# A four-layer network on one core: who makes the inputs of the 64-state scan, and where both scans put their results

## The reference

```python
deltaA = jnp.exp(delta[..., None] * A[None, None])
dBu = delta[..., None] * B_ssm[:, :, None, :] * u[..., None]
_, h = jax.lax.associative_scan(_scan_comb, (deltaA, dBu), axis=1)     # h = deltaA * h_before + dBu
y = jnp.einsum('bldn,bln->bld', h, C_ssm) + u * D_param
```

## Time and profile before

| | us |
|---|---|
| median of the runs | 10314.9 |
| profiled execution | 10319.8 |
| its span | 10318.0 |
| stage two (64-state scan), 2838 to 5845 | 3007 |
| stage four, forward half, 6913 to 8561 | 1648 |
| stage four, backward half, 8561 to 10228 | 1667 |
| VectorE, ScalarE, GpSimd, TensorE busy of the span | 8275.2, 8166.8, 5747.3, 9215.3 |

### The profile page before, as it was taken

One profiled execution on the slowest core, in us unless ns is written; L12 is line 12 of the kernel. 1 busy time (PEld: TensorE's weight loads), 2 busy tenths in 40 slices (PEclk: granted clock), 3 DMA queues, 4 the chain that ended last, 5 costly groups with the idle time before them and its releaser, 6 DMA issues. The chain is left out here.

```text
span 10318.0 us, 146585 instructions
## 1 busy us (share of the span) xinstructions
PE 9215.3 (89%) x50532; PEld 4668.1 (45%) x50532; DVE 8275.2 (80%) x7254; ACT 8166.8 (79%) x15277; POOL 5747.3 (56%) x2628
## 2 busy tenths in 40 slices
PE   9999999999888888888888899988899998888885
PEld 6767767767533333333333344433333333333332
DVE  7858858668499999999999711129999999999997
ACT  5646646556499999999999655569999999999995
POOL 0000000000088888888888500029999999999996
PEclk9999999999899999999999999999999999999997
DMA  0000000000055555555555300015556566656666
GB/s 39 0 1 0 0 1 0 0 0 0 9 182 180 189 183 180 186 182 181 182 184 185 121 8 8 8 63 188 197 193 198 193 199 195 199 193 200 196 196 224
DMA packets 338551, 1249.79 MB, mean 121 GB/s; under 512 B 39280, under 2 KB 39408, under 8 KB 334448
## 3 DMA queue, kind: packets, MB, share of 16 engines
q1 hardware_dynamic: 338032, 1243.13, 37.0%
HBM read 1144.40 MB, written 56.62 MB: 116 GB/s over the span
## 5 line engine op out<-in xcount | busy, mean ns | idle before, releaser
L1905 POOL TENSOR_TENSOR l_ring<-l_ring 128x1024 f32<-128x1024 f32 x1024 | 2450.2, 2422 | 159.0 <-DVE l_ring L1983 158.0
L1001 POOL TENSOR_TENSOR l_hc<-l_h,l_hc 128x1024 f32<-128x1024 f32 x1024 | 2218.1, 2182 | 535.5 <-DVE l_h L1099 517.8
L1983 DVE TENSOR_TENSOR_SCAN l_ring<-l_ring,l_carry,l_ps 128x1024 f32<-128x1024 f32 x960 | 2199.6, 2333 | 0.9
L1099 DVE TENSOR_TENSOR_SCAN l_h<-l_decay,l_h,l_ps 128x1024 f32<-128x1024 f32 x768 | 1755.1, 2333 | 17.0 <-ACT l_decay L873 4.9
L116 POOL COPY l_qm<-l_q 128x128 f32 x128 | 82.4, 646 | 2576.4 <-PE l_ps L188 2179.9
L889 ACT ACTIVATE l_xt<-l_duT,l_BT 128x128 f32<-128x128 f32 x4736 | 1441.2, 388 | 11.1 <-PE l_ps L705 10.9
L1795 ACT ACTIVATE l_xt<-l_duT,l_BT 128x128 f32<-128x128 f32 x4096 | 1247.1, 390 | 0.0
L1587 PE MATMUL l_ps<-l_ring,w_sb 64*64 64x512 f32 x8192 | 1179.1, 648 | 0.8 <-PE l_ps L1587 0.4
L722 PE MATMUL l_ps<-l_hc,w_sb 64*64 64x512 f32 x8192 | 1148.4, 632 | 2.3 <-POOL l_hc L1001 1.8
L212 PE MATMUL l_ps<-l_attnT,l_vT 128*128 128x128 f32 x8192 | 1095.7, 277 | 1.3 <-ACT l_attnT L283 1.3
L212 PEld LDWEIGHTS l_ps<-l_attnT,l_vT 128*128 128x128 f32 x8192 | 1013.9, 192 | 137.8 <-issue 114.7
(11 more groups left out here) (238 smaller groups left out, 14865.6 us busy)
## 6 DMA issues: line engine op xcount, KB each, us to landing
l_hc<-l_rows_dram SPq DMA_DIRECT2D x1024, 512.0 KB, 4.7
l_ring<-l_rows_dram SPq DMA_DIRECT2D x1024, 512.0 KB, 5.1
l_crossed<-l_delta SPq DMA_DIRECT2D x160, 256.0 KB, 3.8
l_gate_dram<-l_gate SPq DMA_DIRECT2D x32, 512.0 KB, 6.6
l_recon_dram<-l_recon SPq DMA_DIRECT2D x32, 512.0 KB, 6.5
l_gate<-l_gate_dram SPq DMA_DIRECT2D x32, 512.0 KB, 5.6
l_xw<-x_dram SPq DMA_DIRECT2D x30, 513.5 KB, 6.8
x_dram<-x SPq DMA_DIRECT2D x16, 512.0 KB, 2.6
```

The lines of the kernel that those rows point to most:

```text
L1001: nc.gpsimd.tensor_tensor(hc[:, unit % CS, :], h[:, unit % HS, window(unit)][:, along(K)], hc[:, unit % CS, :], ALU.mult).then_inc(hc_done, 1)
L1099: nc.vector.tensor_tensor_scan(h[:, unit % HS, window(unit)][:, along(K)], decay[:, unit % DS, :], odd_in if odd else even_in, before, ALU ...
L1905: nc.gpsimd.tensor_tensor(hc[:, unit % CS, :], h[:, unit % HS, :], hc[:, unit % CS, :], ALU.mult).then_inc(hc_done, 1)
L1983: nc.vector.tensor_tensor_scan(h[:, unit % HS, order], decay[:, unit % DS, order], x_now[:, order], before, ALU.mult, ALU.add).then_inc(sc ...
```

## The change

It has these parts.

1. `TURNED` grows from 5 to 14 even units of stage two, whose input ScalarE and TensorE now make instead of TensorE's broadcast and VectorE's multiplication. `BT` grows from 37 to 46 columns.
2. A new list `MADE` names 14 odd units of stage two whose transposed input GpSimd makes, in one operation of 128x1024 (`odd_input`), instead of eight activations on ScalarE. It stands ahead of the two products of the pair before. A semaphore `xt_made` counts them; `xt_ready` counts only ScalarE's.
3. Where a unit's result goes in its slot: in both stages the first column is now 4 (n // 2) + n % 2 plus 1 or 2, so that it is 2 or 3 modulo 4 where the product reads along the positions, and 1 or 2 modulo 4 where it reads in reverse. A slot of `h` has 64 columns more than 1024 in stage two and 32 in stage four.
4. Stage four takes over stage two's way of the carry: `h` is a tensor of its own, results are written forward and in reverse by turns, the next chunk's scan starts from the column that is still there, and `carry`, `keep` and its semaphore go.
5. The scratch space of the software DMA queue is halved, and GpSimd waits once for `taps_ready` (the convolution's taps lie in `xt` until then).

```diff
 DT_AT = PARTS * SEL
-TURNED = (6, 13, 20, 24, 29)
+TURNED = (1, 2, 3, 5, 7, 8, 9, 11, 15, 18, 25, 26, 29, 31)
+MADE = (0, 1, 3, 5, 8, 9, 13, 14, 15, 18, 19, 21, 29, 31)
+FIRST_TURNED = min([(k, 0) for k in TURNED] + [(k, 1) for k in range(S1 // 2) if k not in MADE])
 BTW = SEL + len(TURNED)
...
         rows_dram = nc.dram_tensor("l1_rows_dram", [NCH * S1, CH], F32, kind="Internal").ap()
-        h = sb("h", [128, HS, CH + 2 * USES])
+        h = sb("h", [128, HS, CH + 4 * USES])
         hc = sb("hc", [128, CS, CH])
...
         b_mm = sem("b_mm"); inp_done = sem("inp_done"); xt_ready = sem("xt_ready"); xt_mm = sem("xt_mm")
+        xt_made = sem("xt_made")
         decay_ready = sem("decay_ready"); scan_done = sem("scan_done")
...
             K, q = divmod(unit, S1)
-            first = q // HS if K % 2 else 2 * USES - 1 - q // HS
+            n = q // HS if K % 2 else 2 * USES - 1 - q // HS
+            first = 4 * (n // 2) + n % 2 + (1 if K % 2 else 2)
             return slice(first, first + CH)
...
             return 2 * (P + turned_before(P)) + (2 if odd and P % PAIRS in TURNED else 0)
+
+        def made_before(P):
+            return P // PAIRS * len(MADE) + sum(k < P % PAIRS for k in MADE)
...
                 at_least(pe, scan_done, 2 * P + odd - 1)
+                by_pool = odd and P % PAIRS in MADE
+                if by_pool:
+                    pe.wait_ge(xt_made, made_before(P) + 1)
                 for hf in range(2):
-                    pe.wait_ge(xt_ready, n + hf + 1)
+                    if not by_pool:
+                        pe.wait_ge(xt_ready, n + hf + 1 - 2 * made_before(P))
                     for t in range(4):
...
                 K, k = divmod(P, PAIRS)
-                if k == 0:
+                if (k, odd) == FIRST_TURNED:
                     act.wait_ge(duT_out, 2 * K + 2)
...
             decays(0, 0)
-            turned_input(0, 1, 0)
+            if 0 not in MADE:
+                turned_input(0, 1, 0)
             decays(1, 0)
...
                         decays(2 * P + 2, own)
-                        turned_input(P + 1, 1, own)
+                        if (k + 1) % PAIRS not in MADE:
+                            turned_input(P + 1, 1, own)
                         decays(2 * P + 3, own)
...
+            def odd_input(P, p):
+                K, k = divmod(P, PAIRS)
+                if k == MADE[0]:
+                    pool.wait_ge(duT_out, 2 * K + 2)
+                    pool.wait_ge(bt_ready, K + 1)
+                n = halves_before(P, 1)
+                at_least(pool, xt_mm, n + 2 - XS)
+                into = xt[:, n % XS:n % XS + 2, :].rearrange("p s (t d) -> p (s t) d", d=128)
+                nc.gpsimd.tensor_tensor(into, duT[:, p, :, :], BT[:, p, :, k:k + 1].broadcast_to([128, BLK, 128]),
+                                        ALU.mult).then_inc(xt_made, 1)
+
             squares(0, 0)
...
             input_rate(0, 0)
+            pool.wait_ge(taps_ready, 1)
+            if 0 in MADE:
+                odd_input(0, 0)
             for K in range(NCH):
                     P = K * PAIRS + k
+                    if P + 1 < NCH * PAIRS and (k + 1) % PAIRS in MADE:
+                        odd_input(P + 1, p if k + 1 < PAIRS else 1 - p)
                     product(2 * P)
...
     HS, DS, CS, XS = 4, 4, 8, 4
+    USES = TI * S3 // HS
     ctx = ExitStack()
...
         taps = sb("taps", [128, K3, DI])
-        ring = sb("ring", [128, (HS + DS + CS) * CH])
+        h = sb("h", [128, HS, CH + 4 * USES])
+        ring = sb("ring", [128, (DS + CS) * CH])
         slots = lambda at, n: ring[:, at * CH:(at + n) * CH].rearrange("p (s n) -> p s n", s=n)
-        h, decay, hc = slots(0, HS), slots(HS, DS), slots(HS + DS, CS)
+        decay, hc = slots(0, DS), slots(DS, CS)
         xw = sb("xw", [128, 3, CH + PAD])
...
         loaded = sb("loaded", [128, CH])
-        carry = sb("carry", [128, TI * S3])
         zero = sb("zero", [128, 1])
...
         b_mm = sem("b_mm"); inp_done = sem("inp_done"); xt_ready = sem("xt_ready"); xt_mm = sem("xt_mm")
-        decay_ready = sem("decay_ready"); scan_done = sem("scan_done"); kept = sem("kept")
+        decay_ready = sem("decay_ready"); scan_done = sem("scan_done")
         c_in = [sem(f"c_in_{i}") for i in range(CS)]
...
         forward = lambda K: K < NCH
-
-        def keeps_before(P):
-
-            d, i = divmod(P, NCH * TI * PAIRS)
-            kept_pairs = (NCH - 1) * TI * PAIRS
-            return 2 * (d * kept_pairs + min(i, kept_pairs))
+        in_time = lambda K: forward(K) == (K % 2 == 0)
+
+        def window(unit):
+
+            K, i = divmod(unit, TI * S3)
+            n = i // HS if K % 2 else 2 * USES - 1 - i // HS
+            first = 4 * (n // 2) + n % 2 + (2 if in_time(K) else 1)
+            return slice(first, first + CH)
+
+        def last_column(unit):
+            own = window(unit)
+            return own.start if unit // (TI * S3) % 2 else own.stop - 1
...
                     pool.wait_ge(scan_done, unit + 1)
-                    nc.gpsimd.tensor_tensor(hc[:, unit % CS, :], h[:, unit % HS, :], hc[:, unit % CS, :],
-                                            ALU.mult).then_inc(hc_done, 1)
+                    K = unit // (TI * S3)
+                    along = slice(None) if in_time(K) else slice(None, None, -1)
+                    nc.gpsimd.tensor_tensor(hc[:, unit % CS, :], h[:, unit % HS, window(unit)][:, along],
+                                            hc[:, unit % CS, :], ALU.mult).then_inc(hc_done, 1)
...
                         dve.wait_ge(inp_done, P + 1)
-                        at_least(dve, kept, keeps_before(P - 1) if P else 0)
                     dve.wait_ge(decay_ready, unit + 1)
                     at_least(dve, hc_done, unit - HS + 1)
-                    before = carry[:, e * S3 + q:e * S3 + q + 1] if K % NCH else zero[:]
+                    into = slice(None, None, -1) if K % 2 else slice(None)
+                    at = last_column(unit - TI * S3) if K % NCH else 0
+                    before = h[:, unit % HS, at:at + 1] if K % NCH else zero[:]
                     x_now = odd_in if odd else even_in
-                    nc.vector.tensor_tensor_scan(h[:, unit % HS, order], decay[:, unit % DS, order], x_now[:, order],
-                                                 before, ALU.mult, ALU.add).then_inc(scan_done, 1)
-
-                def keep(unit):
-                    S, q = divmod(unit, S3)
-                    K, e = divmod(S, TI)
-                    at = CH - 1 if forward(K) else 0
-                    dve.wait_ge(scan_done, unit + 1)
-                    nc.vector.tensor_copy(carry[:, e * S3 + q:e * S3 + q + 1], h[:, unit % HS, at:at + 1]).then_inc(kept, 1)
+                    nc.vector.tensor_tensor_scan(h[:, unit % HS, window(unit)][:, into], decay[:, unit % DS, order],
+                                                 x_now[:, order], before, ALU.mult, ALU.add).then_inc(scan_done, 1)
...
                         even_input(P + 1)
-                    if S // TI % NCH < NCH - 1:
-                        keep(2 * P)
-                        keep(2 * P + 1)
                     pieces(S, r)
...
     arrays = {name: _np.ascontiguousarray(a) for name, a in arrays.items()}
-    nc = _bacc.Bacc("TRN2", target_bir_lowering=False, num_devices=1)
+    nc = _bacc.Bacc("TRN2", target_bir_lowering=False, num_devices=1, dynamic_dma_scratch_size=8192)
     args = [nc.dram_tensor(name, a.shape, mybir.dt.from_np(a.dtype), kind="ExternalInput").ap()
```

## The result

The changed kernel takes 10187.5 us (median of 4 runs, 10180.4 to 10189.7) against 10312.0 for the kernel before: 0.9875 of its time, 95% interval 0.9863 to 0.9886. That is 127 us under the 10314.9 that the forecast started from; forecast was 222 us less, and the time lies 2.5 us inside the upper end of the range of 10040 to 10190.

| | before | after | forecast change |
|---|---|---|---|
| stage two | 3006.0 | 2874.8 | -150 |
| stage four, forward half | 1648.1 | 1642.1 | -19 |
| stage four, backward half | 1666.2 | 1672.5 | -53 |

A forecast was written before the change was run, and what follows sets the result against it. VectorE's chain bounds stage two; in stage four ScalarE bounds the forward half and VectorE, with stalls, the backward. 10319.8 - 150 (stage two) - 72 (stage four) = 10097.8, profiled 4.9 above the runs' median, so 10093; range 10040 to 10190.

The forecast's parts named there:

- The products, 1.96 to 2.00 us at the new places: GpSimd, both stages: every product takes the cheap form; stage two's come to 125.4 us a chunk instead of 137.
- The new operation at 1.96 us: GpSimd, stage two: each of 14 odd inputs a chunk costs as much as a cheap product.
- Stage two, 9.4 us a chunk: 64-state scan: 187.9 us a chunk falls to 178.5, saving 150 us over 16 chunks.
- The ideal saving of 11.2: VectorE, stage two: 9 even inputs of 1.25 us leave each chunk, 187.9 to 176.7 us.
- The 1.8 us booked for waits: Stage two, per chunk: 0.3 for TensorE's transposes, 0.5 for late odd inputs, 1.0 for rows of C.
- The wait of TensorE, at most 2.6, goes: Stage four: `du` comes over 2 us sooner from GpSimd, so TensorE no longer waits for it.
- Backward VectorE's own work stays: 1599.4 us: Stage four, backward half: VectorE's busy time is unchanged; with 15 us idle, 1667 - 1614 = 53 us saved.
- rival C: Stage four's places do nothing, something else made products dear; only stage two counts: 10165 us; chance 0.08.
- Stage four, 72 us: Two-way scan: forward half 1648 to 1629 (19 us), backward half 1667 to 1614 (53 us).
- B: GpSimd decides stage two: odd input costs 2.7 us or waits add up; 60 to 95 us saved, 10150 to 10185; chance 0.22.
- the signs: Products 1.96 to 2.00, new operation 1.9 to 2.1, stage two 2850 to 2875, backward near 1614, forward near 1629 us.
- the 7.5 us for k = 1: Stage two: VectorE's time for that pair in the pair-by-pair tally of GpSimd's excess work.

The follow-up runs named there:

- the places alone: Changed kernel with the lists of before (five even inputs turned, no input on GpSimd), keeping new places and carry in h: 10301.3 us, 0.9990 of before.
- the dear places: Changed kernel with stage two's results one or two columns off (0 or 1 modulo 4 even chunks, 3 or 0 odd): 10457.8 us, 1.0142 of before.
- both cures: Changed kernel, stage two's variance and Newton step in PSUM, stage four's GpSimd waiting for VectorE's maximum, gating at r = 6: 10025.8 us, 0.9723 of before.
- the cured kernels: PSUM Newton step plus GpSimd's wait with moved gating, on the kernel before: 10268.2 us (0.9956); on the changed kernel: 10025.8 us (0.9723).
- GpSimd's wait: Changed kernel; stage four's GpSimd waits for VectorE's softplus maximum ahead of r = 3's second product, gating moved to r = 6: 10103.9 us, 0.9802 of before.
- the maximum on GpSimd: Changed kernel; stage four's softplus maximum made by GpSimd in two operations instead of VectorE, gating at r = 6: 10202.6 us, 0.9890 of before.

## Why the prediction was right and where it failed

- The products, 1.96 to 2.00 us at the new places in both stages: right, and shown from both sides by the kernels with the places alone and the dear places. In the kernel before, all 1024 products of stage two follow the place without exception.
- The new operation at 1.96 us: 1.92.
- Stage two, 9.4 us a chunk, was mis-sized but held: 8.0 (188.6 to 180.6, mean of chunks 2 to 13). The ideal saving of 11.2 is there pair by pair. The 1.8 us booked for waits of GpSimd's inputs and for rows did not come in that form: almost every pair stands at 4.50 or 5.74. Four pairs differ. k = 7 lost 4.8 us to the held port, k = 1 lost 1.6 (the sum `y` is late behind more transposes: VectorE waits 21.4 us at L1102, 0 before), k = 8 lost 0.5, and k = 21 gained 3.8, since ScalarE with fewer inputs to make is there in time (VectorE waited 33.0 us in all for its silu before, 2.2 a chunk, now not). No term of the prediction stands for any of these four; the total came near by luck of signs. With both cures the term is 202 us instead of 150, so that the 242 between the cured kernels is near the 222 of the forecast by luck too.
- "The wait of TensorE, at most 2.6, goes": right. The pair r = 6 of stage four went from 7.29 us forward and 7.15 backward (means) to 5.74 in both.
- "Backward VectorE's own work stays: 1599.4 us" failed. It became 1626.8, since the maximum went from mostly 1.44 to 3.05 us (61 of 64 cases); the 31 of the backward half took 94.7 us for 49.7 before. Backward the pair r = 3 went from 7.27 to 8.60 us, and what `du` gave at r = 6, 1.41 us a half chunk, was lost there. The step took the durations of one profile for constants of an instruction, and they depended on when GpSimd's instructions ran. The sign was in the earlier trace rows: products of 2422 ns where the dear place costs 2.36 us, and the prediction noted the difference under rival C and did not follow it up. It is the products held up behind a maximum, 57 of 3.3 to 3.4 us.
- Stage four, 72 us: 0. With GpSimd's wait the changed kernel does reach the forecast's times, 1624.9 and 1602.4 us for 1629 and 1614, so what the term left out is the held port. But 72 us is not what the places are worth by themselves: the kernel before gains 41 us by the same edits, which also move the gating, and the 35 us that remain between the two can all be the port. The waits of `add_y` for the sum, which the prediction did not name, stay: 36 to 62 us in the traces here.
- That the time fell inside the range is luck in part: its upper end stood there for the rivals B and C, and neither has the held port. Rival C has the term of 72 us at nothing, and its time (10165) is nearer than the forecast's, but its mechanism is refuted, since the products of stage four did get cheap. So is that of B (10150 to 10185): the odd input costs 1.92 us, not 2.7, and VectorE stayed 98% busy in stage two.
- Of the signs, products of 2.00 us and an odd input of 1.92 came. Stage two came at the edge (2874.8 us for 2850 to 2875), and the two halves of stage four did not. A smaller slip: the 7.5 us for k = 1 still holds the even input that goes there, 6.2 by the prediction's own rule; it enters only the tally of GpSimd's excess.

The Trainium skill has this. Its page SBUF — State Buffer, section SBUF: two separate sides, says that VectorE and GpSimd have a pair of ports in common, which is locked for a whole instruction and not divided, by whichever starts first: by a GpSimd instruction, or by one of VectorE's that is in a 2-port mode or has two SBUF inputs (the latter only against a GpSimd instruction that reads SBUF). The runs agree: 1.21 us alone, 2.21 with 1.1 us of the other instruction left, 2.66 with 1.6, 3.05 with all of it. It would have put one rival more into the prediction. Where the run with dear places has an 8-element instruction waiting over five GpSimd instructions, "whichever starts first" is not enough; what decides at such a boundary wasn't settled.

## What to carry to other kernels

Before an engine is made denser or its instructions are shifted, list the instructions of the other one that share its port, and price each at the full length of what may be running at least, since some waited over several: here the two cures, for 63 instructions of 1024 columns and 60 of eight, took off 162 us. A duration in a profile is part waiting; look at its spread over the run and beside what the other engine ran at that moment. The cures need no more work of any engine: operands in PSUM, or a wait on the engine that has time.

## What the runs showed of the hardware

- A GpSimd product of two 1024-column f32 operands costs 2.00 or 2.36 us by the first column of its window in `h`, modulo four (the other operand and the result fill a slot from its first column). Read forward, 2 or 3 is cheap; read in reverse, 1 or 2. In the kernel before that holds for all 1024 products of stage two, the cheap ones at 1.98 to 2.06 us and the dear ones at 2.32 to 2.42.
- A GpSimd operation with a repeated operand (one column read 128 times) costs 1.92 us, with the same tensor twice 1.90.
- VectorE's maximum of two SBUF operands takes 1.21 us alone and otherwise what is left of the running GpSimd instruction plus 1.08, but for four cases of the kernel before in which it waited over two more products (6.0 to 6.3 us); the GpSimd product behind it then takes 3.0 us instead of 2.00.
- VectorE's TENSOR_SCALAR from SBUF to SBUF of eight f32 columns waits as the two-operand ones do (1706 ns against 172), and from PSUM to PSUM it does not (175). A COPY of one column from SBUF to SBUF (147 ns) and a BATCH_NORM_STATS2 of 512 columns (0.70 us) don't wait either.
- Beside back-to-back dear products such an eight-column instruction took 8.2 to 9.8 us in 15 cases of 15. Beside cheap ones it mostly took up to 1.9 us, but 5.6 in one case of the changed kernel and in six (5.6 to 6.4) of the one with the maximum on GpSimd.
